# First pass of an attention kernel: tile 3 of both heads split by rows on GpSimd and turned by DMA, and reciprocals without a factor table

## The chip, the cores and the metric

The kernel runs on one core of one Trainium2 chip. The metric is the device time of one execution in microseconds; 888.01 us is the median of three executions of the kernel before (887.39 to 888.87).

## What is computed

A transformer block on 1024 rows of 512 features, all in float32 at the interface: layer norm, then multi-head latent attention (32 heads, 64-wide latent keys and values, 64 rotary features) with a learned top-128 choice of keys for each query, plus a gated mixture of eight low-rank experts; both are added to the input. Cut to the part that this case touches:

```python
scores = (q_nope @ k_nope + q_pe @ k_pe) * QKD ** -0.5   # per head, 1024 x 1024
scores = where(topk_mask & causal, scores, -inf)
attn   = softmax(scores, axis=-1)
out    = attn @ v                                         # per head
x      = x + (out @ o_w) + experts(xn)
```

The kernel folds the key and value projections into the query and output weights, so per head it multiplies probabilities with a 64-wide latent value. Every float32 operand of a product is split into two float16 parts (high, low), and three products are summed.

## The kernel before

The attention loop handles a pair of heads at a time. A "unit" is one pair on one half of the queries: units 0 to 15 are the first pass (queries 0 to 511, causal, so short rows), units 16 to 31 the second pass (queries 512 to 1023). A unit has eight steps: four tiles of 128 queries, each for both heads. Tile t has 128 (t + 1) keys. The order of tiles in the first pass is 3, 0, 2, 1, so steps 0 and 1 of a unit are the widest there (512 keys); in the second it is 7, 4, 6, 5.

Each step g goes through all engines, and each engine's program is written out in a fixed order with semaphores between them:

- TensorE: `scores(g + 3)` (L685), then the transposes of the probabilities of step g ("T", L759), then whatever else the ring of PSUM banks holds at this step ("R" and "L": queries of the unit two ahead, "V": a product of output weights, "O": transposes of a finished unit), then `values` (L712) of an earlier step. `values` of a step whose probabilities TensorE transposed comes two steps later; of a step turned by DMA, LAG = 4 steps later.
- VectorE: `row_max` (L1246) adds the mask and finds the row maximum in one pass; `p_low_chunk` (L1263, its instruction is recorded at the helper's line L1044) makes the low part of the transposed probabilities out of PSUM; `unit_out` (L1269) divides a finished unit by the row sums with a reciprocal (L1272), a multiplication by a table `scaled` (L1274) and a product (L1279). In the first pass VectorE also does the rest of the top-128 search (`top_part`, L1196 and L1203).
- ScalarE: `exp_step` (L985) two steps ahead, `p_hi_chunk` (L996, recorded at the helper's L806) the high part of the transposed probabilities, evacuations of R, L, V and O, and at the end of a unit `rope_hi` (L948) for the unit two ahead, which waits for GpSimd's rotation.
- GpSimd: per unit, in this order: `rope_low` of the next unit (L1500), `rope_cos` of the unit two ahead (L1488, step 3), `rope_sin` (L1493 and L1495, step 5), `vo_low` (L1508, step 6), `q_low` (L1504, step 7). In the second pass also `rows_lo_` (L1510 to L1518): a step that is turned by DMA is split on GpSimd into a float16 high part (a cast, L1515) and a low part (a subtraction, L1517).
- SyncE issues all DMAs from one queue, in program order: `place` (L411, four DMAs that put the next unit's queries in place), `turn` (L442 to L453, the transposing DMA of a split step), `swap` (L401 and L402, two DMAs that exchange even and odd rows for the rotation of the unit two ahead; `rope_sin` waits for them), `load_ow` (L434, L435), `store_vo` (L439) and, in the second pass, `load_vo` (L461).

Steps 1, 3, 5 and 7 of a unit of the second pass (one head) are turned by DMA; in the first pass none is (`TURNED`). `pr` holds the probabilities of four steps in rows of 1024.

## Time and profile before

| | |
|---|---|
| median of 3 executions | 888.01 us (887.39 to 888.87) |
| the profiled execution | 887.79 us, of which the span from first to last instruction is 886.0 us |
| before the attention loop | 0 to about 272 us |
| first pass (units 0 to 15) | about 272 to 497 us |
| second pass (units 16 to 31) | about 497 to 792 us |
| output products | about 792 to 886 us |
| busy share of the span | TensorE 91%, VectorE 76%, ScalarE 67%, GpSimd 60% |

All numbers below are microseconds from the start of the span, unless marked ns. The busy share is a mean over stages with different limits: the first pass is VectorE's stage, the second TensorE's, which the rows by stretch show. In a row of a timeline the first number is the start, the second the duration, and what stands in brackets is the idle time before it and who ended it. An instruction that follows another of its engine at once overlaps it by some 0.05 to 0.1 us, so costs in sequence are read from start to start.

### The profile page before, as it was taken

What the parts mean: (1) busy time and instruction counts of PE and PEld (TensorE: products, weight loads), DVE (VectorE), ACT (ScalarE), POOL (GpSimd) and SP (SyncE); (2) the same over time, 40 slices, a digit from 0 to 9 for tenths busy, and PEclk for the clock granted to TensorE, in tenths of its full rate; (3) what the DMA queues carried; (4) which work ended last, traced back from release to release, by engine and by line L of the source; (5) the groups of instructions that cost most, each with busy time, mean ns of one, the idle gap of its engine ahead of it and who ended that gap; (6) DMA issues with size and microseconds to landing.
All of it is one profiled execution on the core that took longest, in us unless ns stands there. A gap on an engine that the chain in (4) does not pass through costs nothing.

```text
span 886.0 us, 20243 instructions
## 1 busy us (share of the span) xinstructions
PE 804.1 (91%) x7496; PEld 499.8 (56%) x7496; DVE 671.6 (76%) x1557; ACT 596.7 (67%) x1340; POOL 532.6 (60%) x446
## 2 busy tenths in 40 slices
PE   4999989977768888889888999999999999999998
PEld 2565444434435555555555577677677677764443
DVE  6367678899999999999998888888888888851000
ACT  2687889978886878777878667766667676750000
POOL 3177488877874545455554678888887888740000
PEclk9999999989999999999999999999999999999999
DMA  8022211203432444344343387888677677870110
GB/s 257 25 72 74 59 48 48 78 22 95 135 112 92 126 109 136 106 122 126 109 138 101 82 145 135 138 161 158 137 151 144 138 143 155 171 149 28 58 52 31
DMA packets 168786, 96.67 MB, mean 109 GB/s; under 512 B 116720, under 2 KB 142704, under 8 KB 168688
## 3 DMA queue, kind: packets, MB, share of 16 engines
q1 hardware_dynamic: 168688, 95.37, 46.0%
q8 instruction: 60, 0.98, 0.5%
q14 instruction: 38, 0.31, 0.1%
HBM read 36.62 MB, written 6.29 MB: 48 GB/s over the span
## 4 chain that ended last, share of the span: by engine, by line
PE 32%; DVE 21%; POOL 20%; issue 14%; DMA 5%; SPq 4%; ACT 4%; POOLq 0%; DVEq 0%; ACTq 0%
PE psS L775 9%; DVE m L1196 5%; DMA arena<-arena 4%; DVE bias L1203 4%; PE psT L573 4%; DVE arena L1044 3%; SPq L452 3%; DVE arena L1256 3%; PE psS L702 3%; PE psS L586 3%; PE psT L553 2%; PE psS L530 2%; PE psT L759 2%; POOL arena L1517 2%; POOL bias L1470 2%
## 5 line engine op out<-in xcount | busy, mean ns | idle before, releaser
L806 ACT ACTIVATE arena<-psT 128x512 f16<-128x512 f32 (+4 forms) x360 | 172.2, 506 | 108.0 <-PE psT L759 65.9
L702 PE MATMUL psS<-keyT,arena 128*128 128x512 f16 (+3 forms) x1152 | 232.3, 330 | 5.0 <-issue 3.0
L1256 DVE CUSTOM_DVE_ANT_0 arena<-psS,bias 128x512 f32<-128x512 f32 (+7 forms) x256 | 192.1, 752 | 36.3 <-PE psS L702 15.4
L993 ACT ACTIVATE arena<-arena,small 128x512 f32<-128x512 f32 (+7 forms) x256 | 197.5, 774 | 30.5 <-DVE small L1256 29.7
L1044 DVE SCALAR_TENSOR_TENSOR arena<-psT,arena 128x512 f16<-128x512 f32 (+3 forms) x278 | 146.3, 545 | 27.3 <-ACT arena L806 26.7
L759 PE MATMUL psT<-ident,arena 128*128 128x128 f32 x736 | 117.4, 281 | 26.0 <-DVE arena L1044 23.5
L586 PE MATMUL psS<-ikT,big 128*128 128x512 f16 (+3 forms) x528 | 103.9, 341 | 22.9 <-DVE bias L1129 19.4
L702 PEld LDWEIGHTS psS<-keyT,arena 128*128 128x128 f16 x1152 | 92.4, 99 | 56.7 <-issue 7.9
L759 PEld LDWEIGHTS psT<-ident,arena 128*128 128x128 f32 x736 | 85.8, 142 | 59.1 <-ACT arena L993 31.2
L1470 POOL TENSOR_TENSOR bias<-arena,bias 128x768 f32<-128x768 f32 (+2 forms) x48 | 91.4, 1920 | 32.8 <-ACT arena L872 21.7
L586 PEld LDWEIGHTS psS<-ikT,big 128*128 128x128 f16 x528 | 49.5, 100 | 72.0 <-DVE bias L1129 26.8
L1203 DVE MATCH_REPLACE8 bias<-m,bias 128x768 f32<-128x768 f32 (+4 forms) x112 | 90.0, 812 | 0.0
L1196 DVE MAX8 m<-bias 128x8 f32<-128x768 f32 (+4 forms) x112 | 87.5, 817 | 0.5
L1500 POOL TENSOR_TENSOR arena<-arena 128x512 f16<-128x512 f32 x32 | 37.1, 1159 | 73.4 <-ACT arena L806 73.2
L729 PEld LDWEIGHTS psO<-val,arena 128*128 128x128 f16 x1728 | 67.3, 98 | 15.9 <-DVE arena L1044 4.1
L729 PE MATMUL psO<-val,arena 128*128 128x64 f16 x1728 | 71.4, 194 | 0.0
L1493 POOL TENSOR_TENSOR arena<-arena,sq 128x512 f32<-128x512 f32 x32 | 40.8, 1276 | 49.0 <-DMA arena<-arena 49.0
L806 ACT ACTIVATE big<-psT 128x512 f16<-128x512 f32 (+1 forms) x64 | 36.3, 567 | 49.2 <-PE psT L738 32.2
L1044 DVE SCALAR_TENSOR_TENSOR big<-psT,big 128x512 f16<-128x512 f32 (+1 forms) x64 | 41.9, 655 | 29.7 <-ACT big L806 29.3
L806 ACT ACTIVATE arena<-arena 128x512 f16<-128x512 f32 (+1 forms) x112 | 62.7, 591 | 1.0 <-DMA arena<-in_wiq 1.0
L1376 POOL TENSOR_TENSOR arena<-arena 128x512 f16<-128x512 f32 x32 | 37.1, 1162 | 39.1 <-ACT arena L806 39.1
L1129 DVE SCALAR_TENSOR_TENSOR bias<-psS,arena,bias 128x512 f32<-128x512 f32 (+3 forms) x64 | 45.1, 747 | 14.0 <-ACT psS L895 13.5
(164 smaller groups left out, 1384.2 us busy)
## 6 DMA issues: line engine op xcount, KB each, us to landing
arena<-arena SPq DMA_DIRECT2D x192, 128.0 KB, 2.4
arena<-in_wiq SPq DMA_DIRECT2D x32, 256.0 KB, 2.7
arena<-in_ow SPq DMA_DIRECT2D x16, 512.0 KB, 3.5
arena<-in_qbT SPq DMA_DIRECT2D x16, 256.0 KB, 2.5
wvo_parts<-arena SPq DMA_DIRECT2D x16, 256.0 KB, 2.0
arena<-in_qpe SPq DMA_DIRECT2D x16, 128.0 KB, 3.0
arena<-in_x SPq DMA_DIRECT2D x8, 256.0 KB, 3.3
out<-arena SPq DMA_DIRECT2D x8, 256.0 KB, 2.0
```

The costliest lines, as they stand in the source:

```text
L586: last = mm(bank[:, c:c + w], iq[:, a, n, t * P:(t + 1) * P], ikT[:, b, c:c + w], start=(a, b) == (0, 0), stop=(a, b) == (1, 0))
L702: last = mm(bank[:, k:k + w], Q[:, u % 2, h, a, q:q + P], keyT[:, b, h, k:k + w], start=(a, b) == (0, 0), stop=(a, b) == (1, 0))
L729: last = mm(dst, src[:, a, j * P:(j + 1) * P], val[:, b, j, :], start=j == 0 and n == 0, stop=j == nb - 1 and n == 2)
L759: last = nc.tensor.transpose(bank[:, (j % 4) * P:(j % 4 + 1) * P], pr[:, g % 4, j * P:(j + 1) * P], ident[:])
L775: mm(psS[u][:, 0:CH], big[:, a, n, ds(t * P, P)], wvo[n][:, b, :], start=n == 0 and (a, b) == (0, 0), stop=False)
L806: return nc.scalar.activation(dst, src, ACT.Copy, scale=scale)
L993: nc.scalar.activation(pr[:, g % 4, 0:kw], pr[:, g % 4, 0:kw], ACT.Exp, bias=shift[:, g % 4:g % 4 + 1], scale=-1.0, accum_out=rsum[:, unit ...
L1044: return v.scalar_tensor_tensor(out=dst, in0=src, scalar=scale, in1=hi, op0=ALU.mult, op1=ALU.subtract)
L1196: v.max(m8[:, slot], bias[:, TOFF[t]:TOFF[t + 1]]).then_inc(tk_max, 1)
L1203: v.match_replace(out=row, in_to_replace=m8[:, slot], in_values=row, imm_value=TAKEN).then_inc(tk_rep, 1)
L1256: v.tensor_tensor_reduce(out=pr[:, g % 4, 0:kw], in0=bank[:, 0:kw], in1=bias[:, TOFF[t]:TOFF[t + 1]], scale=-c_s, scalar=3e38, op0=ALU.add ...
L1470: g.tensor_tensor(row, src[:, 0:P * (t + 1)], row, ALU.add).then_inc(sum_done, 1)
```

## The change

Steps 0 and 1 of each unit of the first pass (tile 3, 512 keys, both heads) go the way that the odd steps of the second pass go. ScalarE's exponential gets a shift that scales the probabilities by 1024, GpSimd casts and subtracts them by rows, and a DMA from SyncE's queue turns both parts. The eight transposes of TensorE, the two copies of ScalarE and the two subtractions of VectorE for these steps are gone. `values` of these steps comes 6 steps later (`LAGS`). GpSimd's `rows_lo_` of step 0 of a unit stands ahead of `q_low` in step 7 of the unit before; that of step 1 stands behind `rope_low` and ahead of `rope_cos`. SyncE turns step 0 before `place`, and step 1 behind it, ahead of `swap`. Four row buffers and four column buffers of the first pass lie in tiles free at that time, and the probabilities of the first pass have eight buffers of 512 in place of four. At the seam of the passes GpSimd waits for the last four landings. In `unit_out` the first pass scales two columns of the reciprocals by a constant each, in place of one product with a table.

```diff
-LAG = 4
-TURNED = ((), (1, 3, 5, 7))
+LAGS = (6, 4)
+TURNED = ((0, 1), (1, 3, 5, 7))
@@ views
-        pr = view(9856, 4 * S).rearrange("p (u k) -> p u k", u=4)
+        pr_high = view(9856, 4 * S).rearrange("p (u k) -> p u k", u=4)
+        pr_low = view(9856, 8 * CH).rearrange("p (u k) -> p u k", u=8)
+        rows_low = (ikf[:, 0:S], ikf[:, S:2 * S], view(6784, S, F16), view(7296, S, F16))
+        cols_low = [view(at, S, F16) for at in (8832, 9344, 16000, 16512)]
@@ sync
                 sp.wait_ge(row_lo, d + 1)
-                if d == 2:
+                if d >= 4 and d - DMA_LOW < 4:
+                    sp.wait_ge(av_mm, summed(BY_DMA[min(d - 4, DMA_LOW - 1)]))
+                if d - DMA_LOW == 2:
...
                 u, s = divmod(g, 8)
+                if s == 0 and turns(g):
+                    turn(g)
                 if s == 0 and 2 <= u + 1 < NU:
                     place(u + 1, latent, qa_lo, q_lat, 1)
                     place(u + 1, turned, q_rot, q_tur, 0)
-                if turns(g):
+                if s and turns(g):
                     turn(g)
                 if s == 3 and u + 2 < NU:
                     swap(u + 2)
@@ vector
-                if g >= 4 and turns(g - 4):
-                    dve.wait_ge(row_lo, TURN_AT[g - 4] + 1)
-                elif g >= 4:
-                    dve.wait_ge(t_mm, TCUM[g - 3])
+                if half_of(g) == 0:
+                    before = (g - 8,) if g >= 8 else ()
+                else:
+                    before = (2 * g - 8 * NP - 8, 2 * g - 8 * NP - 7) if g < 8 * NP + 4 else (g - 4,)
+                for b in before:
+                    if turns(b):
+                        dve.wait_ge(row_lo, TURN_AT[b] + 1)
+                    else:
+                        dve.wait_ge(t_mm, TCUM[b + 1])
...
-                v.tensor_tensor(rinv, rinv, scaled[:, u // NP], ALU.mult).then_inc(ri_done, 1)
+                if u < NP:
+                    for s in TURNED[0]:
+                        at = rinv[:, col_of(s):col_of(s) + 1]
+                        v.tensor_scalar(at, at, PR_S, None, ALU.mult).then_inc(ri_done, 1)
+                else:
+                    v.tensor_tensor(rinv, rinv, scaled, ALU.mult).then_inc(ri_done, 1)
@@ gpsimd
                 kw, d = P * (tile_of(x) + 1), TURN_AT[x]
-                if d >= 3:
-                    pool.wait_ge(landed[(d - 3) % 4], landed_by(d - 3))
+                if 4 <= d < DMA_LOW:
+                    pool.wait_ge(*landing(d - 4))
+                elif d - DMA_LOW == 0:
+                    for s_, n_ in LAST_LANDED:
+                        pool.wait_ge(s_, n_)
+                elif d - DMA_LOW >= 3:
+                    pool.wait_ge(*landing(d - 3))
                 pool.wait_ge(exp_done, x + 1)
...
+            if turns(0):
+                rows_lo_(0)
             for x in range(STEPS):
                 u, s = divmod(x, 8)
                 if s == 0 and 2 <= u + 1 < NU:
                     rope_low(u + 1)
                 if x + 1 < STEPS and turns(x + 1):
                     rows_lo_(x + 1)
```

## Rows read from the trace of the kernel before

**Rows 1.** Busy by stretch: from:to length, busy (instructions), granted clock, DMA share, GB/s

```profile
400.00:440.00 40.00, 35.44 (x356) 23.12 (x355) 38.19 (x103) 31.82 (x91) 20.95 (x18) 0.96 0.44 125
560.00:640.00 80.00, 79.44 (x1036) 56.34 (x1033) 66.04 (x147) 55.88 (x116) 66.24 (x52) 1.00 0.82 149
```

**Rows 2.** Groups by form, 310 to 480 us: count, busy us, mean ns, idle before

```profile
L806 ACT ACTIVATE arena<-psT 128x512 f16<-128x512 f32 x48 | 28.4, 591 | 10.0 <-PE psT L622 5.6 <-PE psT L709 2.9 <-PE psT L759 0.6
...
L1044 DVE SCALAR_TENSOR_TENSOR arena<-psT,arena 128x512 f16<-128x512 f32 x24 | 16.4, 685 | 0.8 <-ACT arena L806 0.5
...
L1274 DVE TENSOR_TENSOR small<-small 128x8 f32<-128x8 f32 x12 | 6.0, 499 | 0.4
```

**Rows 3.** Groups by form, VectorE, 510 to 790 us (second pass)

```profile
L1261 DVE TENSOR_SCALAR small<-small 128x1 f32<-128x1 f32 x60 | 9.2, 154 | 2.1
```

**Rows 4.** Timeline of VectorE: the outputs of units 0 and 14

```profile
295.21 0.69 DVE L1279 TENSOR_TENSOR arena<-psS,small 128x512 f32<-128x512 f32 x1
...
488.87 0.69 DVE L1279 TENSOR_TENSOR arena<-psS,small 128x512 f32<-128x512 f32 x1
```

**Rows 5.** Timeline of GpSimd, one unit of the first pass

```profile
403.53 1.27 POOL L1493 TENSOR_TENSOR arena<-arena,sq 128x512 f32<-128x512 f32 x1 [1.95 <-DMA arena<-arena]
...
406.23 1.16 POOL L1508 TENSOR_TENSOR arena<-arena 128x512 f16<-128x512 f32 x1
407.34 1.16 POOL L1504 TENSOR_TENSOR arena<-arena 128x512 f16<-128x512 f32 x1
411.92 1.16 POOL L1500 TENSOR_TENSOR arena<-arena 128x512 f16<-128x512 f32 x1 [3.42 <-ACT arena L806]
```

**Rows 6.** Timeline of GpSimd, second pass: splits of 1024 and 640 keys

```profile
591.87 1.16 POOL L1500 TENSOR_TENSOR arena<-arena 128x512 f16<-128x512 f32 x1 [1.11 <-ACT arena L806]
592.97 1.04 POOL L1515 CAST ikT<-arena 128x1024 f16<-128x1024 f32 x1
...
596.17 0.71 POOL L1515 CAST bias<-arena 128x640 f16<-128x640 f32 x1
596.96 1.41 POOL L1517 TENSOR_TENSOR bias<-arena,bias 128x640 f16<-128x640 f32 x1
598.32 1.28 POOL L1488 TENSOR_TENSOR arena<-arena,cq 128x512 f32<-128x512 f32 x1
```

**Rows 7.** Timeline of SyncE's queue: start and time of each issue

```profile
400.78 0.56 SPq L401 DMA_DIRECT2D arena<-arena  x1
...
598.39 1.63 SPq L452 DMA_TRANSPOSE arena<-bias  x1
...
671.43 1.33 SPq L452 DMA_TRANSPOSE arena<-bias  x1
...
727.79 2.99 SPq L452 DMA_TRANSPOSE arena<-bias  x1
730.88 1.36 SPq L452 DMA_TRANSPOSE arena<-arena  x1
732.33 0.64 SPq L401 DMA_DIRECT2D arena<-arena  x1
```

**Rows 8.** Timeline of GpSimd, second pass: starts of the sine product

```profile
604.98 1.28 POOL L1493 TENSOR_TENSOR arena<-arena,sq 128x512 f32<-128x512 f32 x1 [2.53 <-DMA arena<-arena]
...
735.14 1.28 POOL L1493 TENSOR_TENSOR arena<-arena,sq 128x512 f32<-128x512 f32 x1 [1.13 <-DMA arena<-arena]
```

**Rows 9.** Timeline of ScalarE: end of the first exponential, rotation copy at unit 14's end

```profile
273.57 0.19 ACT L993 ACTIVATION_READ_ACCUMULATOR arena<-arena,small 128x1 f32 x1
...
480.37 0.62 ACT L806 ACTIVATE arena<-arena 128x512 f16<-128x512 f32 x1
```

**Rows 10.** Timeline of TensorE: first scores of the second pass, and a gap

```profile
408.56 0.41 PE L759 MATMUL psT<-ident,arena 128*128 128x128 f32 x2 [1.61 <-DVE arena L1044]
...
488.16 2.19 PE L702 MATMUL psS<-keyT,arena 128*128 128x512 f16 x6 [1.98 <-DVE small L1256]
```

**Rows 11.** Busy by stretch, TensorE alone: busy (instructions), granted clock, DMA share

```profile
411.00:412.00 1.00, 1.00 (x6) 0.50 0.01 2
```

More of the change, by code:

```diff
@@ L174, in block_kernel @@
         rbs = small[:, 352:360]
-        nmax = small[:, 360:364]
+        nmax = small[:, 432:440]
         rsum = small[:, 364:380].rearrange("p (v s) -> p v s", v=2)
@@ L238, in block_kernel @@
         av_mm = sem("av_mm"); nmax_done = sem("nmax_done")
-        row_hi = sem("row_hi"); row_lo = sem("row_lo"); landed = [sem(f"landed{j}") for j in range(4)]
+        row_hi = sem("row_hi"); row_lo = sem("row_lo")
+        landed_low = [sem(f"landed_low{j}") for j in range(4)]; landed_high = [sem(f"landed_high{j}") for j in range(4)]
         ri_done = sem("ri_done"); o_done = sem("o_done")
@@ L277, in block_kernel, with pr_of, lag, ri_before @@
         FLIP_AT = {g_: d for d, g_ in enumerate(BY_PE)}
+        PE_LOW = sum(half_of(g_) == 0 for g_ in BY_PE)
+        DMA_LOW = len(BY_DMA) - sum(half_of(g_) for g_ in BY_DMA)
+        assert PE_LOW % 4 == 0 and DMA_LOW >= 4
         def flipped(g):
-            return pT_high[:, FLIP_AT[g] % 2] if half_of(g) else pT_low[:, g % 4]
+            return pT_high[:, FLIP_AT[g] % 2] if half_of(g) else pT_low[:, FLIP_AT[g] % 4]
+        def pr_of(g):
+            return pr_high[:, g % 4] if half_of(g) else pr_low[:, g % 8]
+        def lag(g):
+            return LAGS[half_of(g)] if turns(g) else 2
         def due(x):
-            return [g for g in (x - 2, x - LAG) if 0 <= g < STEPS and turns(g) == (g == x - LAG)]
+            return [g for g in range(max(0, x - max(LAGS)), min(x, STEPS)) if g + lag(g) == x]
         AV_AT = {}
-        for x_ in range(STEPS + LAG):
+        for x_ in range(STEPS + LAGS[1]):
             for g_ in due(x_):
                 AV_AT[g_] = len(AV_AT)
+        def ri_before(u):
+            return (1 + len(TURNED[0])) * min(u, NP) + 2 * max(u - NP, 0)
+        FIRST_AV = [min(range(8 * u_, 8 * u_ + 8), key=lambda g_: AV_AT[g_]) for u_ in range(NU)]
         def summed(g):
@@ L293, in block_kernel, with landing @@
         UNIT_AV = [max(summed(g_) for g_ in range(8 * u_, 8 * u_ + 8)) for u_ in range(NU)]
-        def landed_by(d):
-            return 16 * (d // 4 + 1)
+        def landing(d):
+            return (landed_low[d % 4], 16 * (d // 4 + 1)) if d < DMA_LOW else \
+                (landed_high[(d - DMA_LOW) % 4], 16 * ((d - DMA_LOW) // 4 + 1))
+        LAST_LANDED = [landing(d_) for d_ in range(DMA_LOW - 4, DMA_LOW)]
         def rows_of_turn(d):
-            return rows_high[d % 3]
+            return rows_low[d % 4] if d < DMA_LOW else rows_high[(d - DMA_LOW) % 3]
         def cols_of_turn(d):
-            return cols_high[d % 4]
+            return cols_low[d % 4] if d < DMA_LOW else cols_high[(d - DMA_LOW) % 4]
         RING = []
@@ L786, in _ @@
             experts(0, 0)
-            for g in range(STEPS, STEPS + LAG):
+            for g in range(STEPS, STEPS + LAGS[1]):
                 for late in due(g):
```

40 lines of the change are left out of this document (20 added, 20 removed).

## The prediction

> **What bounds the kernel now.** I read the busy shares by stretch first. In the first pass [rows 1] VectorE is busy 38.19 of 40 us, TensorE 35.44, ScalarE 31.82, GpSimd 20.95; in the second pass TensorE is busy 79.44 of 80. So the stage that the change touches is VectorE's, and GpSimd seems to have half its time free. The change touches the second pass only at its seam, so the question is what one unit of the first pass costs. From the output of unit 0 to that of unit 14 are 193.66 us [rows 4], 13.83 us a unit.
>
> The share of GpSimd hides something, and that is why I then read its timeline and SyncE's. GpSimd works in a fixed order, half of its free time is a wait for a swap DMA (1.95 us) and for ScalarE (3.42 us) [rows 5], and what the change adds stands in that order and in SyncE's. A resource that is free half of the time can still be a ring: a chain of steps in program order in which each unit's first step waits for the last of the unit before.
>
> **What is removed, per unit.** VectorE: two subtractions of 512 at 0.685 us and the product with the table, 0.50 us on average [rows 2]: 1.87 us. It gets four one-column operations (two shifts, two constants), for which the second pass has the row, 0.154 us each [rows 3]: 0.62 us. Net 1.25 us, so that VectorE alone would allow 12.6 us a unit. ScalarE loses two copies, 1.18 us [rows 2] of 31.82 / 40 x 13.83 = 11.0 us, TensorE eight transposes of its 12.3 us. Both stay under 12.6 us. The later `values` cost nothing in work, only place: six steps are 0.75 of a unit, some 10 us, against the 3.7 us of split and issue and some 3 us of landing.
>
> **What is added, per unit.** GpSimd: two pairs of a cast and a subtraction of 512. The second pass has them by start-to-start: a pair of 1024 takes 596.17 - 592.97 = 3.20 us, one of 640 takes 598.32 - 596.17 = 2.15 us [rows 6]; on that line a pair of 512 takes 1.80 us (up to the end of its subtraction 1.85). That is 3.6 us more on 7.2 us. SyncE: two transposing DMAs. Their issue alone holds the queue for 1.33 us at best and 2.99 us at worst [rows 7], and the second one stands ahead of `swap`, for which GpSimd's sine product waits.
>
> **The ring.** In program order, from one sine product to the next one's, nothing here waits for another engine:
> - sine product and sum, to the start of `vo_low`: 406.23 - 403.53 = 2.70 us [rows 5]
> - `vo_low` to the next: 407.34 - 406.23 = 1.11 us [rows 5]
> - split of step 0: 1.80 us
> - `q_low`, the same form as `vo_low`: 1.11 us
> - `rope_low`: 592.97 - 591.87 = 1.10 us [rows 6]
> - split of step 1, to SyncE's issue: 1.85 + 0.02 = 1.87 us (a subtraction ends at 596.96 + 1.41 = 598.37 and the issue starts at 598.39) [rows 6, 7]
> - issue of the transpose, issue of the two swaps and their landing, to the sine product.
>
> The first six are 9.69 us. `rope_cos` runs beside the seventh. The seventh has no row in the first pass, only in the second with 640 keys: 735.14 - 730.88 = 4.26 us at best (five of fourteen cases lie under 4.45) and 604.98 - 598.39 = 6.59 us at worst (seven of fourteen lie over 5.3) [rows 7, 8]. I take 4.3 us, near the best: there each such transpose stands 2 to 3 us behind one of 1024 keys [rows 7], whose data must go first, and in the first pass what stands ahead is 512 wide and some 4 us older. Without a transpose the same stretch is 403.53 - 400.78 = 2.75 us [rows 5, 7], which is the floor if the issue cost nothing. So the ring is **14.0 us a unit**, against 12.6 us for VectorE and 13.83 us now. The bound moves to a ring of GpSimd, SyncE and the swap, and what VectorE gains is lost in waiting.
>
> Could ScalarE break it? The split of step 0 needs an exponential that ScalarE runs two steps ahead, and `rope_low` needs ScalarE's rotation copy, which waits itself for the sine. From the sine's end GpSimd reaches `rope_low` only 1.11 + 1.80 + 1.11 = 4.0 us later, and the copy takes 0.62 us [rows 9]. So the ring closes without ScalarE, which is slack for it.
>
> **The sum.** The ring has a start, too. The first exponential ends at 273.76 [rows 9]; both splits, 1.80 + 1.87 us, follow some 0.1 us later, and with 4.3 us the first sine product starts at 281.9. Fourteen rings later, at 281.9 + 14 x 14.0 = 477.9, starts the one of unit 14, its sum ends 2.6 us later, and ScalarE's rotation copy starts at 480.5, where it now starts at 480.37 [rows 9]. So fourteen units come out at 0.1 us longer: the ring uses up the slack that GpSimd has today. Unit 15 is no longer the ring's: from that copy to the first scores of the second pass are 488.16 - 480.37 = 7.8 us [rows 9, 10], a chain through ScalarE's copies, of which two (1.2 us) go. Together -1.1 us. The second pass and the products behind it keep their work and order; at the seam GpSimd comes from its last sine at about 492 us and has `vo_low`, `q_low` and `rope_low` before the first split of the second pass, as now; the wait for the last four landings is over by then. In the profiled execution's terms 887.8 - 1.1 = 886.7 us; it lies 0.2 us below the median of the runs shown, so I forecast **887 us**. Each 0.1 us more in the ring is 1.4 us in the end.
>
> SyncE's queue: the first transpose stands ahead of `place`, which waits for `q_low` and `rope_low` anyway (1.1 and 2.2 us after the split of step 0), so of its 1.3 us of issue hardly anything is left, and the queries it places are needed only by scores five steps later. The looser reuse of `pr` (eight steps back in place of four) removes a wait that costs nothing in the first pass: `row_max` shows none there.
>
> **What the skill says.** The transpose's issue is 1.36 us of the 4.26 us to the sine, and 2.99 us in a worse row [rows 7, 8]. The Trainium skill, "DMA: Bandwidth & Descriptors", section "Issuing engines are not separate DMA queues", says that the sequencer's time to initiate a DMA is usually small relative to the DMA. By that the seventh step would be the 2.75 us without a transpose, and the ring 12.4 us, under VectorE's 12.6 us. The row speaks against it.
>
> **Rivals.**
> 1. The removal is worth what it seems (the issue is small, or the split is beside the wait). Then VectorE paces at 12.6 us, and 16 units give 16 x 1.25 = 20 us: 868 us. For it: the busy shares, and GpSimd's 3.42 us of wait. Against it: the order of `turn` ahead of `swap` in one queue, and seven rows that add to 9.69 us before the first DMA.
> 2. The ring is longer, **slower than before**: SyncE's issue of a transpose behind `place` takes more than the best case, or the swap queues behind its data. It decides from a seventh step of 4.4 us (a ring of 14.1 us). With the middle of the rows, 5 us, the ring is 14.7 us and the end +8.7 us: 897 us; with the worst, 6.59 us, it is 16.3 us and +31 us: 919 us. For it: an issue of 1.33 us and one of 2.99 us at the same place behind `place` [rows 7], with nothing in the rows that parts them. Against it: those are 1024 wide, twice as much as here.
> 3. TensorE has more room, and its clock falls. After a gap of 1.61 us [rows 10] it is at 0.50 of full speed, its 1.2 GHz level, with nothing idle in that microsecond [rows 11]. It now happens in a few units (granted 0.96 on average [rows 1]). If each unit has such a gap and some 3.5 us at that level, the chain of a unit through TensorE gets some 1.75 us longer, and with VectorE's 12.6 us and its waits it comes to about 14.7 us in place of 14.0: 897 us. Against it: ScalarE's wait is under 1 us a unit in my sum, and VectorE has row maxima to do meanwhile. The Trainium skill, "TensorE: Matmul & The Clock Gate", section "HAM oscillation — how this bites in real kernels", has kernels whose waits throttle the clock in every turn of a loop; that is this rival.
>
> **How the numbers follow.** Forecast (ring of 13.85 to 14.15 us; its floor is the best row less what 128 keys fewer may save, its end the point from which rival 2 begins): 0.52, of which a third is faster by over 0.2% and the rest within; it covers 884.5 to 889. Rival 1: 0.08. Rival 2: 0.32, evenly over rings up to 15.3 us, so nearly all slower. Rival 3: 0.08, slower. About 0.2% is what a measurement of this kernel can tell from no change. That gives faster 0.25, same 0.39, slower 0.36. For the range I leave out rival 1 and the longer third of rival 2 and of its like, that is under 0.2: 884 to 898 us. A gain of more than 4 us is hard to see while the ring stands, so the lower end is close.
>
> **What the profile would show.** VectorE's busy share in the first pass falls from 95% to about 86%, with waits that were not there; ScalarE waits at the rotation copy for GpSimd's sum; GpSimd waits in each unit only ahead of the sine product, and sine products stand 14.0 us apart; SyncE's `turn` of step 1 starts as the split ends. If the sine products are 12.6 us apart, rival 1 holds; if they are over 14.2 us apart and GpSimd waits only there, rival 2, with the issue or the landing as the longer term; if GpSimd waits ahead of `rope_low` for ScalarE and the granted clock is under 0.9, rival 3. The prediction is wrong altogether if the second pass, whose code is the same, changes by more than 1 us.

## The result, and the profile of the kernel after

| | before | after |
|---|---|---|
| median of four runs | 888.07 us (887.39 to 888.87) | 898.34 us (897.26 to 902.55) |
| profiled execution, its span | 887.79 us, 886.0 | 897.28 us, 895.5 |
| mean granted clock of TensorE | 0.987 | 0.981 |

The ratio of the times is 1.0124, with a 95% interval of [1.0089, 1.016]: the kernel after is slower, by 10 us. The forecast was 887 us and the range ended at 898, so both missed. In the two profiled executions the difference is 9.5 us.

Busy time by stretch, after, for one stretch of the first pass and one of the second (columns: stretch, length, busy us of TensorE, its weight loads, VectorE, ScalarE and GpSimd with their instructions, granted clock, DMA share, GB/s), to be laid beside [rows 1]:

```profile
360.00:400.00 40.00, 30.68 (x328) 19.76 (x327) 33.38 (x97) 27.72 (x81) 30.21 (x29) 0.96 0.63 157
560.00:640.00 80.00, 79.02 (x1034) 56.17 (x1034) 65.18 (x145) 55.88 (x116) 64.62 (x52) 1.00 0.78 142
```

VectorE is down from 38.19 to 33.38 of 40 us and TensorE from 35.44 to 30.68; GpSimd is up from 20.95 to 30.21. No engine is full. The second pass is TensorE's as it was. Timeline of GpSimd, after: the sine product, one unit's steps behind it, and the next two sine products, to be laid beside [rows 5]:

```profile
379.59 1.29 POOL L1529 TENSOR_TENSOR arena<-arena,sq 128x512 f32<-128x512 f32 x1 [2.93 <-DMA arena<-arena]
380.95 1.27 POOL L1531 TENSOR_TENSOR arena<-arena 128x512 f32<-128x512 f32 x1
382.30 1.16 POOL L1544 TENSOR_TENSOR arena<-arena 128x512 f16<-128x512 f32 x1
383.40 0.61 POOL L1556 CAST ikT<-arena 128x512 f16<-128x512 f32 x1
384.09 1.16 POOL L1558 TENSOR_TENSOR ikT<-arena,ikT 128x512 f16<-128x512 f32 x1
385.21 1.16 POOL L1540 TENSOR_TENSOR arena<-arena 128x512 f16<-128x512 f32 x1
386.33 1.15 POOL L1536 TENSOR_TENSOR arena<-arena 128x512 f16<-128x512 f32 x1
387.43 0.60 POOL L1556 CAST ikT<-arena 128x512 f16<-128x512 f32 x1
388.12 1.16 POOL L1558 TENSOR_TENSOR ikT<-arena,ikT 128x512 f16<-128x512 f32 x1
389.23 1.26 POOL L1524 TENSOR_TENSOR arena<-arena,cq 128x512 f32<-128x512 f32 x1
393.42 1.27 POOL L1529 TENSOR_TENSOR arena<-arena,sq 128x512 f32<-128x512 f32 x1 [2.93 <-DMA arena<-arena]
...
408.78 1.26 POOL L1529 TENSOR_TENSOR arena<-arena,sq 128x512 f32<-128x512 f32 x1 [4.46 <-DMA arena<-arena]
```

In this unit nothing on GpSimd waits for ScalarE any more; the one wait is for the swap's DMA. The unit takes 13.83 us, the next one 15.36. The chain that ended last, inside 360 to 400 us (start, length, what), goes through the same steps and no others:

```profile
374.28 1.16 POOL arena L1558
375.46 1.29 SPq L476
...
376.85 0.54 SPq L423
...
377.44 2.08 DMA arena<-arena
...
379.59 1.29 POOL arena L1529
```

What the other engines wait for, 330 to 480 us (total, times, longest):

```profile
POOL arena L1529 <- DMA arena<-arena: 34.7, 10, 4.5
...
PE psS L728 <- issue: 27.7, 10, 5.1
ACT arena L832 <- PE psT L785: 24.2, 11, 5.5
DVE arena L1070 <- ACT arena L832: 19.4, 20, 4.4
```

In the same stretch GpSimd waits for ScalarE only once, 0.7 us. TensorE's 27.7 us stand ahead of its scores (L728), once a unit. This view names no releaser there ("issue"), but these scores start 2.0 us behind the end of `place`'s last issue (391.11 behind 389.07, 480.08 behind 478.08), and the profile of `place`'s line names them as waiting for its DMAs. So TensorE waits for the queries that `place` lays down late in the ring, and ScalarE and VectorE wait behind TensorE. The ring paces, and the rest follows; the runs below test that.

Sixteen sine products start at 281.78, 295.62, 309.94, 323.76, 337.73, 351.86, 365.75, 379.59, 393.42, 408.78, 423.42, 438.62, 452.54, 468.58, 482.47 and 497.17. Seven of the fifteen distances lie at 13.82 to 13.92 us and two more at 13.97 and 14.13; six lie at 14.32 to 16.04. That spread is what the runs below had to explain.

### The profile page after: what moved, and what is told of

The parts are those of the page before. It is cut to its first block, busy times and chain, and to the rows that moved or that the text cites. A ratio compares the mean times of both kernels' runs of the same rounds, so it can differ in the third digit from the quotient of the medians.

```text
span 895.5 us, 20061 instructions
## 1 busy us (share of the span) xinstructions
PE 792.6 (89%) x7368; PEld 488.5 (55%) x7368; DVE 654.9 (73%) x1573; ACT 579.7 (65%) x1308; POOL 586.7 (66%) x510
## 4 chain that ended last, share of the span: by engine, by line
POOL 31%; PE 28%; issue 12%; DVE 11%; DMA 9%; SPq 7%; ACT 2%; POOLq 0%; DVEq 0%
PE psS L801 9%; DMA arena<-arena 8%; SPq L476 5%; POOL arena L1531 4%; POOL arena L1529 4%; PE psT L599 3%; POOL ikT L1558 3%; PE psS L728 3%; POOL arena L1558 3%; DVE m L1222 3%; POOL arena L1536 3%; PE psS L612 3%; POOL bias L1506 2%; POOL ikT L1556 2%; PE psT L579 2%
## 5 line engine op out<-in xcount | busy, mean ns | idle before, releaser
L728 PE MATMUL psS<-keyT,arena 128*128 128x512 f16 (+3 forms) x1152 | 235.4, 333 | 47.6 <-issue 41.8
L832 ACT ACTIVATE arena<-psT 128x512 f16<-128x512 f32 (+4 forms) x328 | 153.5, 499 | 148.7 <-PE psT L785 101.7
L1070 DVE SCALAR_TENSOR_TENSOR arena<-psT,arena 128x512 f16<-128x512 f32 (+3 forms) x246 | 124.4, 528 | 51.2 <-ACT arena L832 50.8
L728 PEld LDWEIGHTS psS<-keyT,arena 128*128 128x128 f16 x1152 | 93.4, 99 | 116.9 <-issue 55.6
L785 PE MATMUL psT<-ident,arena 128*128 128x128 f32 x608 | 97.0, 281 | 2.5 <-ACT arena L1019 1.7
L785 PEld LDWEIGHTS psT<-ident,arena 128*128 128x128 f32 x608 | 73.4, 143 | 28.7 <-ACT arena L1019 9.6
L755 PEld LDWEIGHTS psO<-val,arena 128*128 128x128 f16 x1728 | 65.1, 98 | 9.2 <-issue 0.5
L755 PE MATMUL psO<-val,arena 128*128 128x64 f16 x1728 | 68.2, 193 | 0.0
L1412 POOL TENSOR_TENSOR arena<-arena 128x512 f16<-128x512 f32 x32 | 37.1, 1161 | 40.2 <-ACT arena L832 40.2
L1558 POOL TENSOR_TENSOR ikT<-arena,ikT 128x512 f16<-128x512 f32 (+4 forms) x37 | 55.8, 1509 | 3.0
L1558 POOL TENSOR_TENSOR arena<-arena 128x512 f16<-128x512 f32 (+4 forms) x37 | 55.3, 1495 | 3.0
```

The costliest lines, as they stand in the source:

```text
L728: last = mm(bank[:, k:k + w], Q[:, u % 2, h, a, q:q + P], keyT[:, b, h, k:k + w], start=(a, b) == (0, 0), stop=(a, b) == (1, 0))
L755: last = mm(dst, src[:, a, j * P:(j + 1) * P], val[:, b, j, :], start=j == 0 and n == 0, stop=j == nb - 1 and n == 2)
L785: last = nc.tensor.transpose(bank[:, (j % 4) * P:(j % 4 + 1) * P], pr_of(g)[:, j * P:(j + 1) * P], ident[:])
L832: return nc.scalar.activation(dst, src, ACT.Copy, scale=scale)
L1070: return v.scalar_tensor_tensor(out=dst, in0=src, scalar=scale, in1=hi, op0=ALU.mult, op1=ALU.subtract)
L1558: g.tensor_tensor(rows_of_turn(d)[:, kw:2 * kw], pr_of(x)[:, 0:kw], rows_of_turn(d)[:, 0:kw], ALU.subtract).then_inc(row_lo, 1)
```

## The experiments

Each ratio is to the kernel before on the same chip: medians of 887.14, 887.39, 885.89 and 886.89 us in the four groups of runs. Apart from the edits shown each kernel is the one after, whose own time, 898.34 us, comes from yet another group; so differences of a few us between groups are not firm. By "ring" I mean the distance between two sine products, by "landing" the time from the start of the issue of step 1's transpose to the sine product.

### The swap ahead of the transpose

```
                 if s == 0 and 2 <= u + 1 < NU:
                     place(u + 1, turned, q_rot, q_tur, 0)
+                if s == 1 and g < 8 * NP and u + 2 < NU:
+                    swap(u + 2)
                 if s and turns(g):
                     turn(g)
-                if s == 3 and u + 2 < NU:
+                if s == 3 and g >= 8 * NP and u + 2 < NU:
                     swap(u + 2)
```

> The changed kernel, but in the first pass SyncE issues swap(u + 2) ahead of the transpose of step 1 instead of behind it. Work, data and all other orders stay. Theory A (a ring of GpSimd's order, the transpose's issue and the swap's landing paces the first pass): the split of step 1, the transpose's issue and its data leave the ring; what is left is 2.70 + 1.11 + 1.80 + 1.11 + 1.10 us, two issues of place (1.1 us) and 2.75 us of swap, 11.7 us, under VectorE's 12.6 us, so sine products come 12.6 to 13 us apart instead of 14.36, and the whole takes 873 to 880 us. Theory B (TensorE's gaps ahead of the scores of a new unit and its low clock after them pace it): place is where it was, the gaps stay, 895 to 900 us. Theory C (the DMA engines' load paces it): same data, 895 to 900 us.

Measured: 876.58 us (875.75 to 877.69), ratio 0.9877 [0.9838, 0.9915]. One exchange in SyncE's order is worth 22 us and makes the change a gain. Theories B (TensorE's gaps and clock) and C (the DMA load) had 895 us and more, so they fall. The shortest ring is 12.3 us and the mean 12.9. VectorE is busy for 37.65 of 40 us at 360 to 400 and paces again, as the ring theory has it once the ring is shorter than VectorE's work. The ring is not down to what I had summed: `place` and the transpose of step 0 still stand ahead of the swap.

### One head instead of two

```
-TURNED = ((0, 1), (1, 3, 5, 7))
+TURNED = ((0,), (1, 3, 5, 7))
```

> The changed kernel with only step 0 of each unit of the first pass turned by DMA (one head); step 1 goes through TensorE, ScalarE and VectorE as before. No transpose stands between rope_low and swap. Theory A (ring): the ring is 11.7 us as in the run with the swap ahead, and VectorE paces with some 12.9 us a unit (it saves 0.69 us of subtraction and the table product, 0.50, for two one-column operations fewer than after): 873 to 880 us, faster than both kernels. Theory C (DMA load): half of the added data, so about half of the added time, 892 to 894 us. Theory B (TensorE's gaps): between the two kernels as well, 888 to 895 us.

Measured: 878.57 us (877.05 to 879.27), ratio 0.9892 [0.9847, 0.9938]. Half the change gives a gain, the whole of it a loss. Two equal halves of work would not do that; a ring that comes out longer than VectorE's pace only with the second half does. The rings are 12.4 to 15.2 us, most of them 12.4 to 13.6.

### One transpose issued as two

```
-                sp.dma_start_transpose(cols_of_turn(d)[:, 0:2 * nb * P].rearrange("p (j q) -> p j q", q=P),
-                                       rows_of_turn(d)[:, 0:2 * nb * P]).then_inc(landing(d)[0], 16)
+                parts = 2 if d < DMA_LOW and d % 2 else 1
+                n = 2 * nb * P // parts
+                for a in range(0, 2 * nb * P, n):
+                    sp.dma_start_transpose(cols_of_turn(d)[:, a:a + n].rearrange("p (j q) -> p j q", q=P),
+                                           rows_of_turn(d)[:, a:a + n]).then_inc(landing(d)[0], 16)
```

> The changed kernel with the transpose of step 1 of each unit of the first pass issued as two DMAs, one for the high and one for the low part: same data, one more issue of some 1.3 us in SyncE's queue ahead of swap. Theory A (ring, with the issue as a term): 1.3 to 1.4 us more in each of 15 rings, 916 to 921 us, sine products 15.6 to 15.8 us apart. Theory C (only the data count, not the issue): 896 to 901 us. Theory B (TensorE's gaps): place is issued ahead of both, so less than 5 us more.

Measured: 916.83 us (915.59 to 919.35), ratio 1.0333 [1.029, 1.0375]. Timelines of SyncE's queue and of GpSimd in this kernel:

```profile
384.11 2.52 SPq L479 DMA_TRANSPOSE arena<-arena  x2
386.73 0.54 SPq L423 DMA_DIRECT2D arena<-arena  x1
...
389.45 1.27 POOL L1532 TENSOR_TENSOR arena<-arena,sq 128x512 f32<-128x512 f32 x1 [4.14 <-DMA arena<-arena]
```

The same bytes in two issues take 2.52 us of the queue in place of 1.29, the landing is 5.34 us in place of 4.12. The rings without a late landing (explained below) are 15.05 to 15.22 in place of 13.83, and all fifteen have a mean of 15.55 in place of 14.36: the 1.2 us come through. Fifteen rings of 1.2 us are 18 us, and the time is 18 us above the kernel after's first median (16 above its repeat below). It is the number of issues ahead of the swap that costs, not the data. That settles the doubt of rival 1: the issue is no small part of the step.

### The factor table back in place

```
-                if u < NP:
-                    for s in TURNED[0]:
-                        at = rinv[:, col_of(s):col_of(s) + 1]
-                        v.tensor_scalar(at, at, PR_S, None, ALU.mult).then_inc(ri_done, 1)
-                else:
-                    v.tensor_tensor(rinv, rinv, scaled, ALU.mult).then_inc(ri_done, 1)
+                v.tensor_tensor(rinv, rinv, scaled[:, u // NP], ALU.mult).then_inc(ri_done, 1)
```

> The changed kernel with the reciprocals multiplied by a table again (one product of 128x8, which reads two operands from SBUF, in place of two one-column operations with a constant). Theory A (ring): VectorE has some 1.4 us of slack in a unit, so 0.2 to 0.5 us more on it changes nothing: within 2 us of the changed kernel. Rival (VectorE still paces the first pass): 16 times 0.2 to 0.5 us, 3 to 8 us more.

Measured: 902.58 us (898.63 to 903.69), ratio 1.0161 [1.0115, 1.0206]. The kernel after, run again in the second group, gave 900.77 us (899.26 to 902.24), ratio 1.0146 [1.0121, 1.0172]. The table is 4.2 us above the first median of the kernel after and 1.8 above the second, and the intervals overlap: no difference shows, and one of 2 us can't be excluded. What was expected of that repeat:

> The changed kernel itself, beside the next ones on the same chip, to see whether its rings are the same ones again. Expected 896 to 901 us; the first eight rings 13.8 to 14.1 us, six of the last eight 14.6 to 16 us, if the long ones hang on something in the program and not on chance.

The time came as expected. The rings are 13.83, 13.87, 13.82, 14.10, 14.12, 14.02, 13.83 and 15.06 us, then 16.04, 14.07, 14.40, 14.11, 16.33, 14.06 and 14.66: the long ones lie in the later half again, but they are four and not six, and not all in the same units. The 15.06 has a normal landing (4.14 us) and a wait of GpSimd for ScalarE's exponential, 1.15 us.

The same table on top of the first experiment, where VectorE paces:

> The run with the swap ahead of the transpose of step 1, and in addition the table product in place of the two one-column operations in the reciprocals. With the swap ahead VectorE is busy 94% of the pass and near its bound. If VectorE paces there, the product with two operands in SBUF, 0.17 us when alone and 0.5 us on average beside GpSimd in the kernel before, against some 0.2 us for the pair, costs 16 times 0.1 to 0.4 us: 2 to 6 us more than 876.6. If the shorter ring (12.4 us with place) still paces: within 1.5 us.

Measured: 880.04 us (878.19 to 885.74), ratio 0.9927 [0.9905, 0.9949] against 0.9877 [0.9838, 0.9915]. That is some 4 us and inside the 2 to 6 expected, but the intervals overlap and the two were run in different groups. It points to a saving on VectorE that counts where VectorE paces; it does not show it.

### What makes some rings longer

Where a ring takes 13.8 us the DMA view of the stretch from the transpose's issue to the sine product has one queue; where it takes 15.36 us it has packets of two more, which the profile names instruction queues (columns: packets, MB, share of 16 engines; first the 4.1 us before the sine product at 393.42, then the 5.7 us before the one at 408.78):

```profile
q1 hardware_dynamic: 1360, 0.75, 78.4%
...
q1 hardware_dynamic: 1426, 0.89, 87.5%
q8 instruction: 1, 0.02, 1.1%
q14 instruction: 1, 0.01, 0.7%
```

Landings without a `q8` packet are 4.12 to 4.18 us long (4.43 and 5.00 in the two that hold a `q14` packet alone). The five with one are 5.66, 4.81, 5.50, 4.20 and 5.54. In 408.78's ring SyncE's own rows are late as well, 2.00 us for the issue and a longer way to the landing:

```profile
389.30 1.29 SPq L476 DMA_TRANSPOSE arena<-ikT  x1
...
403.12 2.00 SPq L476 DMA_TRANSPOSE arena<-arena  x1
405.22 0.54 SPq L423 DMA_DIRECT2D arena<-arena  x1
```

Is that cause or company? 59 `q8` packets move 0.97 MB in the span, 16 KB each. If they fetch TensorE's program, whose instructions are the most by far, some 128 instructions more ahead of everything should move all of them in time, and the long rings with them:

```
-            pe.wait_ge(ld_id, 16)
+            for _ in range(129):
+                pe.wait_ge(ld_id, 16)
```

> The changed kernel with 128 more waits on a semaphore that has long been reached, at the start of TensorE's program, where it is idle for the first load. They cost nothing there, but all of TensorE's later code lies 128 instructions further on. Theory D (the ring's seventh step, 4.12 us in most units of the changed kernel, is 4.8 to 5.7 us in the units in which a packet of the instruction queue q8 falls between the transpose's issue and the sine product): the packets come at another place of the unit, so other rings are long, and those of the second half of the pass that are long in the changed kernel are mostly not; the end moves by 3 us or more one way or the other, 890 to 906 us. Rival (the late rings are long for what the kernel does there): the same rings are long and the time is that of the changed kernel, within 1.5 us.

Measured: 907.95 us (905.67 to 909.57), ratio 1.0225 [1.0197, 1.0254]. The time is 2 us above the expected range. The packets and the long rings moved together. The rings that were 13.84, 14.32 and 13.82 us are 15.78, 16.03 and 15.85, each now with a `q8` packet in its landing (6.07, 6.31, 6.14 us), and a landing of 4.13 us returns in the ring after them, which has none. In the later half the expectation held in part: three rings that had a packet are without one, and two that had landings of 4.20 and 4.18 us have 5.39 and 5.55. The DMA view and GpSimd's timeline of the second of these:

```profile
q8 instruction: 1, 0.02, 0.9%
```

```profile
318.99 1.27 POOL L1530 TENSOR_TENSOR arena<-arena,sq 128x512 f32<-128x512 f32 x1 [5.12 <-DMA arena<-arena]
```

The traces of all thirteen runs behind the change bear it out. From the start of the swap's first issue to the sine product are 208 stretches. 137 hold neither a `q8` nor a `q14` packet, and 136 of these are 2.66 to 2.85 us long (one is 4.27, with an issue of 2.08 us). 38 hold a `q8` packet: 32 of them are 3.28 to 4.94 us, six are 2.77 to 3.02. The 33 with a `q14` packet alone are 2.65 to 3.62. So a late swap goes with a packet, and moving the code moves both; that a packet costs almost nothing in six rings suggests that its exact place counts. Why one packet of 16 KB holds the swap up by up to 2 us is not shown, and neither is what the packets fetch.

Not all of this kernel's loss is that. The expectation that the added waits cost nothing was wrong: TensorE's first transposes start at 11.83 us instead of 7.75 in the repeat. Of the 7.2 us between the medians some 4 are this start, and some 3 are left for the rings. The fifteen rings add to 221.7 us against 216.3 in the repeat; a shorter way from the last of them to the second pass gives part of that back.

### Place ahead of both transposes

Is it really the ring, and not TensorE's gaps (rival 3)? Here `place` goes ahead of the transposes, which was meant to serve TensorE, and both transposes stand together ahead of the swap, which hurts the ring:

```
                 u, s = divmod(g, 8)
-                if s == 0 and turns(g):
-                    turn(g)
                 if s == 0 and 2 <= u + 1 < NU:
                     place(u + 1, turned, q_rot, q_tur, 0)
-                if s and turns(g):
+                if turns(g):
                     turn(g)
```

> The changed kernel with SyncE's four place issues ahead of the transpose of step 0, and both transposes ahead of swap. The queries of a new unit land 1.3 us earlier, for which TensorE waits 2.75 to 5 us in each unit; but the transpose of step 0 is now still in SyncE's queue when the split of step 1 ends: its issue starts 1.15 us behind the end of rope_low and takes 1.25 us, that split ends 1.8 us behind it, so the transpose of step 1 and swap go out 0.6 us later. Theory A (ring): 0.6 us in 15 rings, 9 us more, 906 to 910 us. Theory B (TensorE's gap ahead of the new unit's scores paces the pass): 1.3 us less in each unit, 880 to 890 us.

Measured: 914.16 us (913.32 to 914.35), ratio 1.0297 [1.0262, 1.0332]. Seven of the ten rings without a `q8` packet are 14.79 to 14.84 us, 0.99 more than after's (the other three 14.94 to 15.18). The time is above the 906 to 910 us expected, as the ring's loss is above the 0.6 us expected. SyncE's timeline shows why:

```profile
318.36 2.40 SPq L433 DMA_DIRECT2D arena<-arena  x4
320.86 2.69 SPq L476 DMA_TRANSPOSE arena<-arena  x2
323.64 0.54 SPq L423 DMA_DIRECT2D arena<-arena  x1
```

The four issues of `place` start as `q_low` ends (318.33), and the two transposes follow without a gap, though the split of step 1 has ended at 321.25. From the end of `q_low` to the swap are 5.3 us in place of 4.3 in the kernel after. The other half of the edit did little: the last issue of `place` ends 9.19 us behind the sine product in place of 9.48, 0.3 us earlier and not 1.3, as `place` had been waiting for `q_low` and `rope_low` before. So this run confirms the ring but hardly tests rival 3. The run with the swap ahead does: there `place` kept its position, TensorE's clock is 1.00 at 360 to 400 us, and 22 us are gained.

### Both transposes behind the swap

```
                 u, s = divmod(g, 8)
-                if s == 0 and turns(g):
-                    turn(g)
                 if s == 0 and 2 <= u + 1 < NU:
                     place(u + 1, turned, q_rot, q_tur, 0)
+                if s == 1 and g < 8 * NP:
+                    swap(u + 2)
+                    turn(g - 1)
+                    turn(g)
-                if s and turns(g):
+                if g >= 8 * NP and turns(g):
                     turn(g)
```

> As the run with the swap ahead, and the transpose of step 0 of each unit of the first pass moved too: SyncE issues place, swap, then both transposes. In the run with the swap ahead the ring is still 12.4 us, since the transpose of step 0 holds place back by 1.3 us (place has 2.45 us of issues behind it). Without that the ring is 11.7 us. If that ring still took part in the pace: 2 to 8 us less than 876.6, 869 to 875 us. If VectorE alone paces: within 1.5 us of 876.6. The values of step 0 are due six steps later, 9 us, so its later transpose should cost nothing.

Measured: 874.27 us (871.43 to 874.7), ratio 0.9837 [0.9807, 0.9868]. Timelines of SyncE's queue and of GpSimd:

```profile
391.26 0.54 SPq L423 DMA_DIRECT2D arena<-arena  x1
...
392.54 2.65 SPq L476 DMA_TRANSPOSE arena<-arena  x2
...
394.00 1.27 POOL L1531 TENSOR_TENSOR arena<-arena,sq 128x512 f32<-128x512 f32 x1 [1.13 <-DMA arena<-arena]
```

The swap goes at 391.26, the 2.65 us of issue follow it, beside work, and GpSimd's wait is 1.13 us in place of 2.93. The rings are 12.7 us in the mean and VectorE is busy for 38.30 of 40 us: it paces close to the 12.6 us of the prediction. The median is 2.3 us under the run with the swap ahead, at the edge of the 2 to 8 expected of a ring that still takes part; the intervals overlap, so that these 2 us are real is not shown.

### The seam: two masks beside GpSimd

At the start of the second pass VectorE applies two masks, and it took longer than it did before. Timelines of the kernel before, and then of the one after, VectorE's row first in each:

```profile
492.03 1.22 DVE L1213 TENSOR_SCALAR bias<-bias 128x1024 f32<-128x1024 f32 x2
...
488.84 1.16 POOL L1508 TENSOR_TENSOR arena<-arena 128x512 f16<-128x512 f32 x1
493.91 1.17 POOL L1504 TENSOR_TENSOR arena<-arena 128x512 f16<-128x512 f32 x1 [3.91 <-ACT arena L806]
```

```profile
499.10 2.73 DVE L1239 TENSOR_SCALAR bias<-bias 128x1024 f32<-128x1024 f32 x2
...
499.85 1.49 POOL L1544 TENSOR_TENSOR arena<-arena 128x512 f16<-128x512 f32 x1
501.31 1.53 POOL L1540 TENSOR_TENSOR arena<-arena 128x512 f16<-128x512 f32 x1
```

Before, GpSimd stood still between 490.0 and 493.91, and the pair took 1.22 us. After, it works beside the masks; they take 2.73 us, and GpSimd's own rows 1.49 and 1.53 in place of 1.16. In the kernel with both transposes behind the swap GpSimd is idle beside the pair again, and the pair takes 1.22 us (at 476.06). The Trainium skill, "SBUF — State Buffer", section "Who interferes with whom", has VectorE and GpSimd share a pair of ports that one of them holds for a whole instruction, and names `tensor_scalar` among the operations that can take it. These rows agree.

Moved to two steps of the last unit of the first pass:

```
                 if g == 8 * NP:
-                    for t in GROUPS[2]:
-                        mask(t)
                     dve.wait_ge(mask_done, 7)
                     ...
+                if g in (8 * NP - 8, 8 * NP - 6):
+                    mask(GROUPS[2][(g - 8 * NP + 8) // 2])
```

> The changed kernel with the two masks of the long rows (1024 and 896 wide, ahead of the first row maximum of the second pass) moved up to steps 0 and 2 of the last unit of the first pass, where VectorE waits 0.9 and 1.9 us. In the changed kernel the pair takes 2.73 us, 1.22 us in the kernel before: GpSimd works beside it now (vo_low and q_low, 1.49 and 1.53 us in place of 1.16), it did not before. Theory E (this is 1.5 us of the added time, and the pair stands on the path at the seam): 1.5 to 3 us less than the changed kernel, which is 897 to 901 us. Rival (the path at the seam goes elsewhere, through placing the queries and TensorE): within 1 us.

Measured: 898.18 us (895.45 to 899.26), ratio 1.0123 [1.0081, 1.0164]. By its time this kernel can't be told from the one after. Its profile can say more. From the first scores of the second pass to the first row maximum of 1024 keys are 499.63 - 496.81 = 2.8 us, in the kernel after 501.86 - 494.76 = 7.1 us, and from that row maximum to the last output are 311.1 and 310.8 us. So the 4.3 us saved at the seam reach the end, but for 0.4: VectorE is on the path there. 2.7 of them are the masks. The other 1.5 are TensorE's clock: its six matmuls for these scores, behind a wait of 2.33 us in both kernels, take 2.66 us at a granted clock of 0.50 after, and 1.46 us at 1.00 here. What hides the gain is the first pass: the sine product of unit 14 starts 1.6 us later than after's, with five late landings of 5.36 to 5.99 us where that one has four. TensorE's timeline in this kernel, and its clock (columns: stretch, length, busy, granted clock, DMA share, GB/s), first here, then after:

```profile
496.81 1.46 PE L728 MATMUL psS<-keyT,arena 128*128 128x512 f16 x6 [2.33 <-DVE small L1287]
```

```profile
497.00:498.00 1.00, 1.00 (x6) 1.00 0.77 199
```

```profile
496.00:497.00 1.00, 1.00 (x4) 0.50 0.03 4
```

Both together, both transposes last and the masks early:

> Both transposes behind swap, as in the run with the turns last, and the masks moved up. In that run the pair of masks takes 1.22 us, so at most that much comes off 874.3: 872.5 to 874.5 us, if VectorE at the seam is on the path; more than 874.5 if the masks now stand in the way of unit 15's work.

Measured: 870.57 us (868.87 to 871.45), ratio 0.9805 [0.977, 0.984]. Busy time by stretch, and the masks on VectorE's timeline:

```profile
360.00:400.00 40.00, 34.18 (x353) 21.13 (x350) 38.33 (x114) 32.06 (x92) 34.22 (x33) 1.00 0.72 169
```

```profile
466.76 1.05 DVE L1241 TENSOR_SCALAR bias<-bias 128x1024 f32<-128x1024 f32 x1
```

It is the fastest version of the study: 15 us under the kernel before in this group and close to the 868 us of rival 1. It came out lower than I expected, though it shared no group with the kernel of the experiment before, and the intervals overlap. The two profiles, whose spans are 3.3 us apart (872.9 and 869.6), put 2.7 us at the seam: from the scores to the row maximum are 5.5 us there and 2.8 here. 1.2 of these are the masks, and the rest is TensorE's clock again (six matmuls of 2.72 us at 0.50 there, 1.46 us at 1.00 here).

### The shift on the best version

The 128 waits of the shift, on top of the version just shown:

> Both transposes behind swap and the masks moved up (870.6 us, ratio 0.9805), with the 128 extra waits at the start of TensorE's program that made the changed kernel 7 us slower. Theory D (the late landings cost time only where the ring paces): here the ring is 11.7 to 12 us beside VectorE's 12.6, so a landing later by 1 to 2 us in a few units is taken up in part: ratio 0.979 to 0.985, within 3 us. Rival (the shift costs TensorE time by itself, fetches or waits at bad places): ratio 0.986 to 0.990, 5 to 8 us more, as in the changed kernel.

Measured: 879.22 us (876.02 to 879.85), ratio 0.9917 [0.9886, 0.9948]. This was a miss: with the ring slack I expected the shift to cost under 3 us. The rival, that the shift costs time by itself, had 5 to 8 us and is nearer. TensorE's timeline names half of it. First row in the best version, then with the shift:

```profile
7.84 1.94 PE L548 MATMUL psT<-ident,big 128*128 128x128 f32 x8 [7.84 <-DVE big L1094]
```

```profile
11.88 1.94 PE L549 MATMUL psT<-ident,big 128*128 128x128 f32 x8 [11.88 <-issue]
```

The 128 waits, though satisfied, put the start of the kernel off by 4.04 us. That is at least 32 ns each: without them TensorE waits for VectorE until 7.84, so some of them ran in time that was idle anyway. The rest of this execution keeps its distance: the first sine product is 4.4 us later, the last output 4.6 us, the span 4.6 us. So in the profiled execution the shift costs next to nothing behind its own start. But it is no test of theory D, as no `q8` packet falls in a swap of it. The best version has one, a swap of 4.19 us, in a ring of 14.31 us that is 12.88 with the shift. So a late landing seems to cost time where the ring is just under VectorE's pace too; one ring doesn't show it. The medians, however, are 8.6 us apart. The three other executions have spans of 877.2 to 878.0 us at granted clocks of 0.988 to 0.99 where the profiled one has 874.2 us at 0.994. What those 3 us more are is open, since only the profiled execution can be read.

## Why the prediction was wrong, point by point

**The mechanism was right.** The bound moved from VectorE to the ring of GpSimd, SyncE's issue and the swap. GpSimd waits almost only ahead of the sine product, the chain of waits runs through these steps, and the runs that shorten or lengthen one step of the ring move the time with it, in both directions.

**The first six steps were right.** 9.69 us were summed; a ring of 13.83 us less its landing of 4.12 is 9.71. The start was right, too: the first sine product was put at 281.9 and starts at 281.78. VectorE's saving held, as the versions with a short ring pace at 12.7 to 12.9 us against the 12.6 summed.

**The step that failed is the seventh**, from the issue of step 1's transpose to the sine product. I gave it one value, 4.3 us, "near the best". Its mean over the fourteen rings up to unit 14 is 4.52 us, so the ring is 14.3 us and not 14.0. Undisturbed the step is better than forecast, 4.12 us. But four of the fourteen have a landing of 4.81 to 5.66 us with a `q8` packet in it, 5.0 us together over 4.12. All fourteen together are 3.1 us over the forecast; another 1.5 us of ring are mostly two waits of GpSimd for ScalarE's exponential, 0.41 and 0.73 us (ended at 299.89 and 457.13), from which I had thought the ring free. The sine product of unit 14 starts at 482.47 where I had 477.9: 4.6 us of the 10.6 by which the profiled execution is above its forecast of 886.7. The wide spread of that stretch in [rows 7, 8] was the sign. I read it as a question of width, best or worst, and not as a time that varies from unit to unit, whose mean counts in a ring.

**ScalarE was not slack.** In the sum its rotation copy starts as the ring's sum ends, 480.5. It starts at 487.61, that is 7.1 us later, 4.6 of them the ring's and 2.5 its own. Timelines of ScalarE and TensorE, after, to be laid beside [rows 9, 10]:

```profile
487.61 0.62 ACT L832 ACTIVATE arena<-arena 128x512 f16<-128x512 f32 x1
```

```profile
480.08 0.81 PE L728 MATMUL psS<-keyT,arena 128*128 128x512 f16 x3 [4.06 <-issue]
...
494.76 2.66 PE L728 MATMUL psS<-keyT,arena 128*128 128x512 f16 x6 [2.33 <-DVE small L1287]
```

The queries placed late in the ring reach TensorE's scores late (4.06 us of waiting). Then TensorE's granted clock is at 0.50 from about 481.2 to 484.6, and matmuls of 512 columns start 0.43 us apart in place of 0.22. ScalarE's copies stand behind those. I had followed `place` only for what it costs SyncE, and had said that its queries are needed five steps later. So the gap and the low clock that rival 3 feared are there, behind the ring and not in place of it.

**The seam lost more.** From the rotation copy to the first scores of the second pass are 494.76 - 487.61 = 7.15 us, 0.6 less than the 7.8 before; I had taken 1.2 off. The two masks cost 1.5 us more, and the run that moved them shows VectorE on the path there. No step of mine had that, as I looked at what GpSimd does at the seam but not at who works beside it. Another 0.5 us is TensorE's clock: the six matmuls of these scores take 2.66 us in place of 2.19. The row maximum behind them is at 501.86 against 493.28, which is 8.6 us.

**The second pass** is 0.9 us longer (last outputs at 812.61 and 803.09, 9.5 us apart), inside the 1 us that I had allowed.

In one line, in us: forecast -1.1, rings +4.6, ScalarE behind the ring +2.5, unit 15 +0.6, masks +1.5, clock at the seam +0.5, second pass +0.9: together the 9.5 that lie between the two profiled executions.

**The rivals.** The side was rival 2's, and so is the size: its condition, a seventh step over 4.4 us, is met by the mean of 4.52. Its first reason is not borne out, a longer issue of the transpose behind `place`: that takes 1.28 to 1.31 us in every ring but two (2.00 and 1.94). Its second, a swap that queues behind the transpose's data, isn't either: undisturbed the swap takes 2.72 to 2.79 us from its issue to the sine product, against 2.75 without a transpose ahead of it [rows 5, 7]. Rival 1's 868 us were out of reach for this order of SyncE's queue and within 3 us for another one. Of the signs named beforehand, "sine products over 14.2 us apart and GpSimd waits only there" came true in the mean (14.3 up to unit 14), and VectorE's share fell to 83%, not 86. ScalarE's waits stood at its copies behind TensorE rather than at the rotation copy.

**The chances.** 0.36 for slower was the share of rivals 2 and 3, and the range left out the longer third of rival 2. Drawn by that rule, with rings up to 14.9 us, it would have ended at some 899 us and just held the result; I drew it at 898. The mean of the seventh step over the fourteen units of [rows 7, 8] is 5.3 us, which gives a ring of 15.0 and some 900 us: on the right side, though with a step that is longer than the 4.52 it came to.

## What to carry to other kernels

Before work goes to an engine that looks half idle, close the loop of what runs there in program order with its DMA issues and landings, and compare its length with the pace of the bound: here 14 us against 12.6 turned 20 us of possible gain into a loss. Size such a loop by the mean of its landings, since it pays each late one in full and gets nothing back. In a queue's order, put the transfer that someone waits for ahead of the one that has time: that one exchange was worth 22 us, and with the other transpose behind the swap and the masks moved it was 28.

## What the runs showed of the hardware

- The DMA engines also carry the instruction queues' packets, at moments that the kernel doesn't choose. A swap took 2.66 to 2.85 us to the sine product in 136 of 137 cases without such a packet, and 3.28 to 4.94 us in 32 of 38 with a `q8` packet of 16 KB. When 128 instructions were put ahead of TensorE's program, late swaps came in units that had none before.
- Issuing a transposing DMA of 1024 columns takes mostly 1.23 to 1.31 us of SyncE's queue (2.00 and 1.94 in two rings), one half as wide just as long (2.52 us for two), an issue of the swap 0.54 to 0.60.
- 128 semaphore waits, all satisfied, put TensorE's start off by 4.0 to 4.2 us, in part of which it would have been idle.
- Two masks on VectorE beside GpSimd's subtractions took 2.73 us in place of 1.22, and GpSimd's subtractions 1.49 and 1.53 in place of 1.16.
- Behind the same wait of 2.33 us TensorE's clock was 0.50 in one kernel and 1.00 in another; six matmuls took 2.66 and 1.46 us.
